# A graph network on one core: own rows fetched earlier, one float32 product in place of three float32r products, the clamp moved to VectorE, and a new order on TensorE

## The reference, cut to what matters

```python
def _gcn_conv(x, W, b, src, dst, dinv):
    h = x @ W
    norm = dinv[src] * dinv[dst]
    agg = segment_sum(h[src] * norm[:, None], dst, num_segments=x.shape[0])
    agg = agg + (dinv * dinv)[:, None] * h
    return agg + b

deg = segment_sum(ones, dst, n) + 1.0
dinv = rsqrt(deg)
x = _l2norm(_gcn_conv(x, W1, b1, ...))           # 128 -> 256
def f(z):
    z1 = _l2norm(_gcn_conv(z, Wf1, bf1, ...))    # 256 -> 256
    return _gcn_conv(z1, Wf2, bf2, ...) + z      # 256 -> 256
k1 = f(x); k2 = f(x + 0.5 * k1); k3 = f(x + 0.5 * k2); k4 = f(x + k3)
x = x + (k1 + 2.0 * k2 + 2.0 * k3 + k4) / 6.0
x = _gcn_conv(x, W2, b2, ...)                    # 256 -> 128
x = layernorm(x_in + x)
x = layernorm(x + attention_layer(x, edges))
```

## Time and profile before

| | |
|---|---|
| median of 3 runs | 9843.62 us (9836.4 to 9845.99) |
| the profiled execution | 9828.63 us, of which the span is 9826.9 us |
| busy, share of the span | PE 68%, VectorE 72%, GpSimd 59%, ScalarE 33% |
| mean granted TensorE clock | 0.841 |

### The profile page before, as it was taken

One profiled execution on the slowest core, in us unless ns is written; L12 is line 12 of the kernel. 1 busy time (PEld: TensorE's weight loads), 2 busy tenths in 40 slices (PEclk: granted clock), 3 DMA queues, 4 the chain that ended last, 5 costly groups with the idle time before them and its releaser, 6 DMA issues. The chain is left out here.

```text
span 9826.9 us, 182033 instructions
## 1 busy us (share of the span) xinstructions
PE 6644.3 (68%) x40144; PEld 5541.6 (56%) x40144; DVE 7056.7 (72%) x18358; ACT 3281.2 (33%) x9311; POOL 5751.9 (59%) x7213
## 2 busy tenths in 40 slices
PE   2500899999998445866777686778666779944654
PEld 0100888888897334655666565666555665523543
DVE  3900777777887556889879887988899882256766
ACT  0000666666675233521441153125100112201333
POOL 0077787888823777854674486458322657700877
PEclk9655999999998556999998898889777878855999
DMA  9333356444443445878779888988898653333433
GB/s 138 83 104 102 123 132 123 132 129 130 132 139 122 116 115 157 237 231 254 225 228 287 258 240 245 291 248 237 264 283 260 194 168 86 86 89 102 143 108 95
DMA packets 1940450, 1679.40 MB, mean 171 GB/s; under 512 B 180872, under 2 KB 1851529, under 8 KB 1940021
## 3 DMA queue, kind: packets, MB, share of 16 engines
q1 hardware_dynamic: 1513269, 1094.63, 39.1%
q0 software_dynamic: 160192, 335.62, 12.5%
q10 hardware_dynamic: 266560, 244.12, 7.3%
HBM read 1049.96 MB, written 624.08 MB: 170 GB/s over the span
## 5 line engine op out<-in xcount | busy, mean ns | idle before, releaser
L1187 PE MATMUL bank<-c_rows,c_sums 128*128 128x256 f32 (+1 forms) x3920 | 1473.6, 463 | 1538.1 <-DVE c_rows L1278 1370.0
L1187 PEld LDWEIGHTS bank<-c_rows,c_sums 128*128 128x128 f32 x3920 | 698.0, 222 | 1881.1 <-DVE c_rows L1278 1593.1
L1141 POOL DMA_INDIRECT c_rows<-t_tab,src_row x784 | 869.9, 1110 | 1198.7 <-PE bank L1187 1042.1
L1220 ACT ACTIVATE c_hi<-bank 128x512 fp32r<-128x512 f32 (+1 forms) x980 | 554.8, 566 | 2549.3 <-PE bank L1197 2549.2
L1278 DVE SCALAR_TENSOR_TENSOR c_rows<-bank,carry,c_rows 32x256 f32<-32x256 f32 (+1 forms) x1950 | 913.2, 468 | 305.0 <-PE bank L1187 182.6
L1141 POOL DMA_INDIRECT c_rows<-z_tab,src_row x784 | 799.4, 1020 | 303.4 <-issue 176.3
L947 DVE TENSOR_TENSOR lx_lo<-bank,lx_hi 128x512 fp32r<-128x512 f32 (+1 forms) x1000 | 658.2, 658 | 352.2 <-ACT lx_hi L892 322.4
L669 PE MATMUL bank<-wf_hi,c_hi 128*128 128x256 f32 x3136 | 838.2, 352 | 19.6 <-DVE c_lo L1307 19.6
L1307 DVE TENSOR_TENSOR c_lo<-bank,c_hi 128x512 fp32r<-128x512 f32 (+1 forms) x980 | 638.2, 651 | 286.8 <-ACT c_hi L1220 284.1
L1298 DVE SCALAR_TENSOR_TENSOR c_u<-bank,lead,c_own 128x256 f32<-128x256 f32 x1764 | 759.8, 469 | 0.3 <-issue 0.2
L669 PE MATMUL bank<-wf_hi,lx_hi 128*128 128x256 f32 x3200 | 710.4, 303 | 61.1 <-issue 34.1
(11 more groups left out here) (303 smaller groups left out, 18082.7 us busy)
## 6 DMA issues: line engine op xcount, KB each, us to landing
c_z<-z_tab SPq DMA_DIRECT2D x882, 256.0 KB
c_sums<-sum_tab SPq DMA_DIRECT2D x980, 128.0 KB
z_tab<-lz SPq DMA_DIRECT2D x400, 256.0 KB
t_tab<-lt SPq DMA_DIRECT2D x400, 256.0 KB
z_tab<-y ACTq DMA_DIRECT2D x392, 256.0 KB
c_own<-z_tab SPq DMA_DIRECT2D x392, 256.0 KB
t_tab<-y ACTq DMA_DIRECT2D x392, 256.0 KB
c_own<-t_tab SPq DMA_DIRECT2D x392, 256.0 KB
```

The lines of the kernel that those rows point to most:

```text
L1141: pool.indirect_dma_start(out=rows[:, s, i, 0:XW] if first else rows[:, s, i, :], out_offset=None, in_=source, in_offset=bass.IndirectOffs ...
L1187: nc.tensor.matmul(psum[s % 2][:, i * win:(i + 1) * win], sums[:, s, i, :], rows[:, s, i, 0:win], start=True, stop=True).then_inc(S["summe ...
L1220: nc.scalar.activation(x_hi[:, s % 2].rearrange("p k n -> p (k n)")[:, 0:n], psum[2 + s % 2][:, 0:n], ACT.Copy).then_inc(S["high"], 1)
```

## The change

Four things change, all around `coupled_stage`.

1. The own rows of the 25,000 slots are fetched in the local pass: GpSimd gathers one tile in 8 of a block's 40 slots (`gather_own`), SyncE stores it to `xo_tab` (`store_own`), and `edge_tables` pauses in as many slots. "first" loads them from `xo_tab` with one plain DMA for each pair.
2. The coupled products use float32 throughout: `c_xt` (the transposed rows, copied once by ScalarE) times the unsplit weight (`full_product`). VectorE's `low` is gone. The local pass keeps its three products.
3. In first and mid the factor `dinv` goes into the scale of ScalarE's square (`c_root_deg`), so `invert` on GpSimd is the power alone; the clamp is a `clamp` step on VectorE of lag 5 ahead of `take`. "first" works out two small tables for it (`c_root_deg`, `c_least`) in `add_own`.
4. TensorE's order in a turn becomes sum 0, product of tile 0, sum 1, transposes, product of tile 1.

```diff
+def full_product(nc, out, x, w, ks):
+    for k in range(ks):
+        last = nc.tensor.matmul(out, x(k), w[:, k, :], start=(k == 0), stop=(k == ks - 1))
...
 # local_pass
+        own_slots = [2, 6, 12, 16, 22, 26, 32, 36]
...
-                    next(tables, None)
+                    if q not in own_slots:
+                        next(tables, None)
...
+                def gather_own(b, q, odd):
+                    if q not in own_slots:
+                        return
+                    k = own_slots.index(q)
+                    t = b * 8 + k
+                    if t >= TE:
+                        return
+                    if t >= 4:
+                        pool.wait_ge(S[f"xo_out{k % 4}"], 16 * (t // 4))
+                    pool.indirect_dma_start(
+                        out=xo[:, k % 4, :], out_offset=None, in_=m["x_tab"],
+                        in_offset=bass.IndirectOffsetOnAxis(ap=m["own_row"][:, t:t + 1], axis=0)
+                    ).then_inc(S[f"xo_in{k % 4}"], 16)
...
-                staggered(pool, blocks, Q, early, [(5, invert)], unrolled=True)
+                staggered(pool, blocks, Q, early, [(0, gather_own), (5, invert)], unrolled=True)
...
-                staggered(sp, blocks, Q, early, [(0, load), (8, load_again), (16, store)])
+                    sp.wait_ge(S[f"xo_in{k % 4}"], b * 32 + 16 * (k // 4 + 1))
+                    sp.dma_start(m["xo_tab"].rearrange("(t p) c -> p t c", p=P)[:, bass.ds(b * 8 + k, 1), :],
+                                 xo[:, k % 4:k % 4 + 1, :]).then_inc(S[f"xo_out{k % 4}"], 16)
+                staggered(sp, blocks, Q, early, [(0, load), (3, load_again), (14, store_own), (16, store)])
...
 # coupled_stage, SyncE and GpSimd
+                if first:
+                    sp.dma_start(own[:, s, :, 0:XW], tiles(m["xo_tab"], j, XW)).then_inc(S[f"own_in{s}"], 16)
...
-            if first:
-                steps.append((3, store_x))
...
-                if first:
-                    for i in range(2):
-                        t = j * 2 + i
-                        pool.indirect_dma_start(
-                            out=own[:, s, i, 0:XW], out_offset=None, in_=source,
-                            in_offset=bass.IndirectOffsetOnAxis(ap=m["own_row"][:, t:t + 1], axis=0)
-                        ).then_inc(S[f"{own_in}{s}"], 16)
...
-                    nc.gpsimd.tensor_scalar(ss[:, s, :], ss[:, s, :], L2_EPS ** 2, None, ALU.max
-                                            ).then_inc(S["clamped"], 1)
...
-                    nc.gpsimd.tensor_tensor(inv[:, s, :], inv[:, s, :], dinv[:, bass.ds(j * 2, 2)], ALU.mult
-                                            ).then_inc(S["inverted"], 1)
...
 # TensorE
+            def multiply(i):
+                def step(j, s):
+                    if i == 0:
+                        pe.wait_ge(S["copied"], ph.at("copied", j))
+                        if past(j, 2):
+                            pe.wait_ge(S["taken"], ph.at("taken", j - 2))
+                    full_product(nc, psum[4 + s % 2][:, i * wout:(i + 1) * wout],
+                                 lambda k: xt[:, s % 2, k, i * P:(i + 1) * P], m[w + "_w"], ks
+                                 ).then_inc(S["product"], 1)
+                return step
-            skewed(pe, pairs, [(0, add_up(0)), (2, turn), (0, add_up(1)), (3, multiply)])
+            skewed(pe, pairs, [(0, add_up(0)), (3, multiply(0)), (0, add_up(1)), (2, turn), (3, multiply(1))])
...
 # ScalarE
                     last = nc.scalar.activation(m["c_squares"][:, i, :], y[:, s, i, :], ACT.Square,
+                                                scale=m["c_root_deg"][:, bass.ds(j * 2 + i, 1)],
                                                 accum_out=ss[:, s, i:i + 1])
...
 # VectorE, add_own in "first"
+                    v.reciprocal(root_deg, own[:, s, :, D + 1]).then_inc(S["rows_known"], 1)
+                    dve.wait_ge(S["rows_known"], ph.at("rows_known", j, 1))
+                    v.scalar_tensor_tensor(least, root_deg, L2_EPS ** 2, root_deg, ALU.mult, ALU.mult
+                                           ).then_inc(S["rows_known"], 1)
...
+            def clamp(j, s):
+                if final:
+                    dve.wait_ge(S["chain"], ph.at("chain", j))
+                    v.tensor_scalar(ss[:, s, :], m["c_mv"][:, s, :, 1], LN_EPS, None, ALU.add
+                                    ).then_inc(S["clamped"], 1)
+                else:
+                    dve.wait_ge(S["squared"], ph.at("squared", j))
...
+                    v.tensor_tensor(ss[:, s, :], ss[:, s, :], m["c_least"][:, bass.ds(j * 2, 2)], ALU.max
+                                    ).then_inc(S["clamped"], 1)
...
-            steps = [(0, carry_on(0)), (1, add_own), (3, low), (0, carry_on(1)), (4, take)]
+            steps = [(0, carry_on(0)), (1, add_own), (0, carry_on(1)), (4, take)]
+            if rooted:
+                steps.insert(len(steps) - 1, (5, clamp))
```

More of the change, by code:

```diff
@@ L226, in gnn_kernel @@
     max_line = dram("max_line", [HEADS, SLOTS])
-    xo_tab = dram("xo_tab", [SLOTS, D])
+    xo_tab = dram("xo_tab", [SLOTS, XW])
     ident = sb("ident", [P, P])
@@ L636, in _ @@
                 for n, (name, ks, width, _) in enumerate(parts):
-                    last = nc.scalar.activation(m[name + "_hi"][:, 0:ks, :], w_in[:, n, 0:ks, 0:width], ACT.Copy)
+                    last = nc.scalar.activation(m[name + "_hi"][:, 0:ks, :], m[name + "_w"][:], ACT.Copy)
                 last.then_inc(S["w_hi"], 1)
@@ L839, in store, with store_own @@
                                  target[c][:, h, :, :]).then_inc(S[out_name(h, store_class(c))], 16)
-                staggered(sp, blocks, Q, early, [(0, load), (8, load_again), (16, store)])
+                def store_own(b, q, odd):
+                    if q not in own_slots:
+                        return
+                    k = own_slots.index(q)
+                    if isinstance(b, int) and b * 8 + k >= TE:
+                        return
+                    sp.wait_ge(S[f"xo_in{k % 4}"], b * 32 + 16 * (k // 4 + 1))
+                    sp.dma_start(m["xo_tab"].rearrange("(t p) c -> p t c", p=P)[:, bass.ds(b * 8 + k, 1), :],
+                                 xo[:, k % 4:k % 4 + 1, :]).then_inc(S[f"xo_out{k % 4}"], 16)
+                staggered(sp, blocks, Q, early, [(0, load), (3, load_again), (14, store_own), (16, store)])
+                for k in range(4):
+                    sp.wait_ge(S[f"xo_out{k}"], 16 * (TE // 4))
                 for odd in range(2):
@@ L1071, in coupled_stage @@
     n_rest = [1, 1, 1, 4][r] + 1 if end else 1 if final else 0
-    own_in = "own_gathered" if first else "own_in"
     ph = counts.phase(pairs, {
-        "gathered*": 32, own_in + "*": 32 if first else 16, "sums_in*": 16,
+        "gathered*": 32, "own_in*": 16, "sums_in*": 16,
         "others_in*": 16 * len(others), "scaled": 2 if first else 0, "carried": 2, "summed": 2,
-        "own_scaled": 1 if first else 0, "u_set": 1, "turned": 1, "high": 1, "low": 1,
-        "product": 1, "taken": 1, "rest_set": n_rest, "squared": 1 if normed else 0,
+        "own_scaled": 1 if first else 0, "u_set": 1, "turned": 1, "copied": 1,
+        "product": 2, "taken": 1, "rest_set": n_rest, "squared": 1 if normed else 0,
         "chain": 2 if final else 0, "clamped": 1 if rooted else 0,
-        "inverted": (2 if normed else 1) if rooted else 0, "done": 0 if end else 1, "stored*": 16,
-        "stored_too*": 16 if first else 0})
+        "inverted": 1 if rooted else 0, "rows_known": 2 if first else 0, "done": 0 if end else 1, "stored*": 16})
     done = "taken" if end else "done"
@@ L1214, in _, with copy @@
             n = ks * H2
-            def high(j, s):
+            def copy(j, s):
                 act.wait_ge(S["turned"], ph.at("turned", j))
@@ L1239, in store @@
                 act.dma_start(tiles(target, j, wout), y[:, s, :, 0:wout]).then_inc(S[f"stored{s}"], 16)
-            steps = [(2, high)]
+            steps = [(2, copy)]
             if normed:
```

67 lines of the change are left out of this document (20 added, 47 removed).

## The result

| | before | after |
|---|---|---|
| median, us | 9844.53 (4 runs, 9836.4 to 9845.99) | 9382.44 (4 runs, 9374.65 to 9394.97) |
| ratio, 95% interval | | 0.9533 [0.9517, 0.955] |
| profiled execution, its span, us | 9828.63, 9826.9 | 9394.97, 9393.2 |
| mean granted TensorE clock | 0.841 | 0.883 |

The kernel is 462 us faster. The forecast was 9205: the gain is 177 us short of it, and the range (9030 to 9400) holds the time by 18 us. Of the nine executions of the kernel before that were taken beside e9 to e11, one took 18525 us at a mean granted clock of 0.443, and is left out of every comparison. The stages tell where the 177 us went. Here are the windows of the kernel after, by stage; columns and order are those of the earlier trace rows, with the local pass ahead.

The account below looks back on a forecast made before the run. GpSimd was taken to bound the mid stages, VectorE the end stages. The terms -272 - 125 - 236 - 40 + 36 = -637 turned the profiled 9829 us into 9192, given as a median of 9205; range 9030 to 9400.

Parts of the forecast that it names:

- "first": Stage "first": gathers, clamp and product leave GpSimd, VectorE then counts at 3.95 us a pair; 684 to 412 us, -272.
- "last": Stage "last": VectorE loses work, its waits for TensorE stay in part; 4.5 us a pair, -40 (bounds -15 and -75).
- Mid stages: Four mid stages: each pair falls from 3.87 to 3.55 us; -125 in all (bounds -235 and 0).
- the forecast's own sign: Mid stages: the forecast called itself wrong if they stay at 3.87 us a pair.
- The ring: Mid stages: a two-turn chain of waits through TensorE, ScalarE and VectorE ends last; 7.04 us, 3.52 a turn, taken as 3.55.
- The order: End stages: one product of 0.88 us between the sums fills TensorE's wait for carry 1, so the new order helps.
- End stages: Four end stages: VectorE loses `low`, part lost to slower loads near 336 GB/s; -66, -55, -55, -60, together -236.
- The float32 product: Coupled stages, TensorE: four float32 products at 0.44 us, 1.76 against 1.61 for twelve float32r; 0.15 us more a pair.
- Local pass: Local pass: 196 added gathers keep indirect DMAs going to its end, slowing the stretch without tables; +36 (bounds +15 and +110).
- half-speed clock: Rival, 1 in 25: TensorE becomes the bound at half its clock in the coupled stages; about 10730 us, slower than before.
- The rival in which neither ring nor ceiling binds: Rival, 1 in 7: mid stages at GpSimd's 3.27, end stages down by the full `low`; -235 and -280, 9050 us.
- The rival in which less comes back: Rival, 1 in 4: end stages gain only 160, mid stages half (-60), the local pass loses 90; 9401 us.

Follow-up runs that it names:

- e9: The changed kernel, unaltered, run once more beside e10 and e11: 9377.42 us, 0.9527 of the kernel before.
- e11: e10 with VectorE's clamp moved behind `take`: 9068.24 us, 0.9211 of the kernel before.
- e5: The kernel before with only the own rows moved (gathered in the local pass, loaded plainly in "first"): 9760.66 us, 0.9752 of the kernel before.
- e1: The changed kernel with VectorE's clamp moved behind `take`: 9421.5 us, 0.9391 of the kernel before on that chip.
- e2: The changed kernel with the clamp of first and mid back on GpSimd, ahead of the power: 9413.64 us, 0.9384 of the kernel before.
- e3: The changed kernel with TensorE's old order (sum, transposes, sum, both products), float32 products kept: 9428.69 us, 0.9398 of the kernel before.
- e7: The changed kernel with TensorE's order first sum, transposes, product of tile 0, second sum, product of tile 1: 9294.81 us, 0.9284 of the kernel before.
- e10: The changed kernel with the edits of e7 and e8 together: 9085.98 us, 0.9228 of the kernel before.
- e8: The changed kernel with each own gather in the skipped table step's place, behind the inverse root, store lag 19: 9514.0 us, 0.9505 of the kernel before.

## Why the prediction was right, and where it was wrong

The time lies in the range, and the parts that carry the gain, "first", the end stages and "last", came within 30 us of their terms. One part came with the wrong sign, and that the sum still fell 18 us inside a range of 370 is partly luck. The terms below are compared by the profiled executions: 9192 forecast, 9395 measured, 203 us apart (the medians are 177 apart, since this execution lies 13 us above its own median).

**"first": -272 forecast, -242 measured.** The own rows do all of it (e5). The forecast took VectorE for the new bound at 3.95 us a pair; it was busy for 354 of 442 us, and the same ring as in the mid stages set 4.3, since the edits that shorten that ring shorten "first" as well: 408 in e1, 402 in e2, 415 in e3. With the clamp on GpSimd it takes 402, with the order of e7 and the clamp behind `take` 400.

**Mid stages: -125 forecast, +29 measured** (by the windows 408, 404, 406 and 407 against four times 399). This is the step that failed, and it makes 154 of the 203 us; by the forecast's own sign ("It is wrong if mid stages stay at 3.87") this part was wrong, for they came at 3.92. GpSimd was relieved as foreseen, to 262 us busy. The ring "Sum 7.04, so 3.52 a turn" was the right mechanism with the wrong size: 7.84, so 3.92. The bound for no gain was "0.3 us more a turn than I see", and it had 0.4. Piece by piece, forecast against measured: second sum to transposes 0.44, 0.53; to the copy 0.65, 0.73; copy to scale 0.57, 0.49; scale and the gap to the first square 1.56, 1.73; squares to the clamp 1.02, 1.22; clamp 0.2, 0.21; `take` 0.79, 0.83; carry 0 and `add_own` to carry 1 1.26, 1.55; carry 1 to sum 0.55, 0.55. Three of them make 0.66 of the 0.80. Carry 1 waits 0.29 for the first sum, which itself waits for carry 0: a wait inside the ring that the forecast, adding up only VectorE's work, left out. The squares and what follows take 0.20 more. ScalarE reads its accumulator behind the second square until 3858.78, so its part is 1.10 where 1.02 was priced: the scale from a tensor costs two squares 0.18, not 0.10. The 0.12 from there to the clamp's start is the signal from ScalarE to VectorE, which the sum had put at nothing. The gap between the scale and the first square, in which ScalarE issues the store, makes 0.17. That the ring binds, and not a single engine, is shown by e1, e2, e3 and e7: each cuts or shortens it elsewhere and gets 26 to 57 us a stage with the work of the engines unchanged, or in e2 with more on GpSimd.

**The order.** The forecast said "The new order helps there", of the end stages. It doesn't: 413, 439, 439 and 643 in the old order, 414, 441, 441 and 644 in the new. In the mid stages it costs 31 us each against the old order, and 57 against e7.

**End stages: -236 forecast, -235 measured**, but by errors that cancel. The first fell by 55 (forecast 66), the second and third by 67 and 60 (55 each), the fourth by 53 (60). The loss to slower loads that the forecast put into the second and third did not come: the second moved its 141 MB at 320 GB/s. The 336 GB/s of the earlier trace rows was what the kernel before asked for in ten microseconds, and no ceiling; the changed kernel moves more in such a stretch (length, busy times, clock, DMA share, GB/s as in the earlier trace rows):

```profile
4990.00:5000.00 10.00, 7.93 (x40) 6.39 (x41) 9.56 (x22) 1.27 (x3) 5.18 (x5) 1.00 1.06 358
```

The first stage, where only 4 us were taken off for that, got back 0.56 us a pair of `low`'s 0.71; where the other 0.15 went isn't settled.

The Trainium skill (DMA: Bandwidth & Descriptors, Bandwidth, Measured) gives 425 GB/s for a core that loads 16 MB at once. This kernel reaches 320 at a DMA share of 0.98, so its mix of row gathers, loads and stores fills the DMA engines well below that figure; the most that any trace here shows in ten microseconds is 368, in e11 from 4710 to 4720 us.

**"last": -40 forecast, -49 measured** by the table (494 to 445). Right.

**The float32 product** was priced at 0.44 for each matmul of 256 columns. In e3, where all four follow each other with the next sum right behind, they take 3903.09 - 3901.37 = 1.72, so 0.43 each. The Trainium skill (FP8 and Floating Point Precision, TensorE Precision Notes) has four passes for true float32. By an estimate from that, four products of four passes against twelve of one would be a third more; the measured 1.72 against 1.61 is 7% more, so these traces don't agree with that estimate. They give the ratio of the times alone, 3.2 for one product, and not the number of passes.

**Local pass: +36 forecast, +46 measured**, and +28 in e9. The windows give +58, but 12 of it belong to preparation: the first load of the pass starts at 1002.41 before and at 1014.70 after. Why preparation is longer, which the forecast called untouched, stays open. The chips and executions spread by more than the term (2179 to 2225). The size was met by luck, for the mechanism was wrong: indirect DMAs run to the end of the pass as it said, but e10 has as many and takes 2149, no more than the 2152 before. What costs is how the own gathers share the slots: with the edit of e8 the pass is 31 us shorter on the same chip (e9, e10), 0.16 for each of the 196 gathers, of which the forecast said that "each is paid back 5 slots on". Why e10 loses nothing against before, with DMAs in slots that had none, stays open.

**The rivals.** No half-speed clock came: the granted clock rose, in the second end stage from 0.85 to 0.97, in "last" from 0.79 to 0.95. TensorE was busy for a larger share of the second end stage (75% for 70%), but for a smaller one of "last" (61% for 77%). The rival in which neither ring nor ceiling binds had -235 for the mid and -280 for the end stages; neither came, though no ceiling at 336 showed, and with e7's order the mid stages reach -198. The rival in which less comes back gave 9401, near the time, but by other terms: its lost end stages did not happen, and its mid stages still gained half.

## What to carry to other kernels

When an engine is relieved, add up the ring that is next to it from a timeline with the waits that its links have for each other, and not from busy times: 0.80 us in two turns, more than half of it in three links, turned a gain of 125 us into a loss of 29. A small instruction that waits for another engine is not priced by its own length. On GpSimd the clamp cost 0.32 us a pair (e2); in VectorE's queue it cost 0.65 over GpSimd's own 3.27 in the changed order of TensorE, and next to nothing in the order of e7, where what it waits for comes early enough (350 us a mid stage, and 348 with the clamp behind `take`, e11). And the order on a shared engine is tried in more than two forms: here it paid to put what feeds the longest way round early in the turn, and to let one product, not two, stand last.

## What was unexpected of the hardware

- The DMA engines held 320 GB/s at a share of 0.98 over a whole stage of 442 us, with 358 in ten microseconds of it, and VectorE waited there for TensorE 6 times, for 14.1 us together (before 29 times, 22.1 us).
- A square of 128x256 with its scale read from a tensor takes 0.51 and 0.49 us, where the plain one took 0.42, and the gap from the scale to the first square is 0.83 in place of 0.65.
- TensorE's granted clock rose in the second end stage from 0.85, busy for 357 of 509 us, to 0.97, busy for 330 of 442. In "last" it rose from 0.79 to 0.95 although the engine was busy for a smaller share. What raised it was not tried.
- The kernel before took 9844 to 10033 us on different chips (medians), and the difference lay mostly in preparation and in attention with what follows.
